# Logits of a mixture-of-experts gate from eight extra columns of the output projection, in a decoder block on one Trainium2 core

## The reference

```python
y = _layer_norm(x + _mha(x, Wqkv, bqkv, Wo, bo), g1, be1)
z = _layer_norm(y + _moe(y, Wg, W1, b1, W2, b2), g2, be2)
...
logits = xf @ Wg.T              # xf: the rows of y
idx = jnp.argmax(logits, axis=-1)
for e in range(E):
    m = (idx == e)[:, None].astype(xf.dtype)
    h = jax.nn.relu(xf @ W1[e] + b1[e])
    out = out + m * (h @ W2[e] + b2[e])
```

## Time and profile before

| | us |
|---|---|
| median of 3 runs | 1223.05 (1222.92 to 1227.51) |
| the profiled execution, its time | 1222.52 |
| the profiled execution, its span from the first to the last instruction | 1220.8 |
| TensorE busy in the span | 1124.4 (92%) |
| VectorE / ScalarE / GpSimd busy | 727.6 / 483.6 / 500.4 |
| mean granted TensorE clock | 0.983 of full speed |

### The profile page before, as it was taken

How to read it: one execution, slowest core, us unless ns; L and a number is a source line. 1 busy time by engine, 2 the same in 40 slices (tenths; PEclk the granted TensorE clock), 3 DMA queues, 4 the chain that set the end, 5 groups by cost and what they waited for, 6 DMA issues and landing times. The chain is left out here.

```text
span 1220.8 us, 29847 instructions
## 1 busy us (share of the span) xinstructions
PE 1124.4 (92%) x10228; PEld 768.5 (63%) x10237; DVE 727.6 (60%) x2056; ACT 483.6 (40%) x863; POOL 500.4 (41%) x721
## 2 busy tenths in 40 slices
PE   8999999999999999999898889888889999999995
PEld 3545455464554644645554455666657999999994
DVE  4555666757766677565725556554565655656553
ACT  5444454445454545445352233322213333333330
POOL 3334425244252443442432222343243566556664
PEclk9999999999999999999999999998979999999998
DMA  7266654644637345364372132348013111111110
GB/s 222 71 186 160 173 155 115 184 111 121 188 105 210 88 143 163 89 192 136 80 203 74 53 105 88 114 136 290 20 41 103 48 46 52 49 53 52 52 44 7
DMA packets 142614, 137.97 MB, mean 113 GB/s; under 512 B 29512, under 2 KB 135886, under 8 KB 142416
## 3 DMA queue, kind: packets, MB, share of 16 engines
q1 hardware_dynamic: 136944, 124.20, 35.4%
q0 software_dynamic: 5280, 12.66, 3.1%
q10 hardware_dynamic: 320, 0.16, 0.1%
HBM read 49.37 MB, written 50.83 MB: 82 GB/s over the span
## 5 line engine op out<-in xcount | busy, mean ns | idle before, releaser
L970 ACT ACTIVATE probs<-ps_ab 128x512 f32<-128x512 f32 (+2 forms) x352 | 174.5, 537 | 92.4 <-PE ps_ab L1292 36.5
L591 POOL TENSOR_SCALAR_AFFINE_SELECT probs<-probs 128x512 f32<-128x512 f32 x128 | 81.9, 640 | 267.0 <-ACT probs L970 263.0
L2810 PE MATMUL ps_ab<-e_yT,e_w_now 128*128 128x128 f32 x1248 | 145.8, 275 | 0.0
L2810 PEld LDWEIGHTS ps_ab<-e_yT,e_w_now 128*128 128x128 f32 x1248 | 142.5, 192 | 0.1
L2821 PE MATMUL ps_c<-keep_w,e_hT 128*128 x624 | 141.0, 379 | 0.0
L2821 PEld LDWEIGHTS ps_c<-keep_w,e_hT 128*128 128x128 f32 x624 | 115.7, 190 | 14.1
L712 DVE CUSTOM_DVE_ANT_0 ps_ab<-ps_ab,mask_qk 128x256 f32<-128x256 f32 x224 | 88.9, 450 | 18.9 <-PE ps_ab L1261 18.8
L706 DVE TENSOR_REDUCE top<-ps_ab 128x2 f32<-128x512 f32 (+1 forms) x112 | 74.1, 683 | 28.4 <-PE ps_ab L1261 27.5
L2745 DVE TENSOR_SCALAR e_hT<-ps_ab,keep_b 128x128 f32<-128x128 f32 x312 | 84.4, 343 | 7.5 <-PE ps_ab L2810 4.6
L1261 PE MATMUL ps_ab<-k_rows,q_rows 96*128 96x256 bf16 (+1 forms) x512 | 84.5, 260 | 4.6 <-DVE top L712 2.7
L1820 ACT ACTIVATE e_w_now<-keep_w 128x1024 f32 x78 | 78.1, 1049 | 22.2 <-issue 12.3
(11 more groups left out here) (236 smaller groups left out, 2120.8 us busy)
## 6 DMA issues: line engine op xcount, KB each, us to landing
sorted_rows<-filler SPq DMA_DIRECT2D x8, 4290.0 KB, 16.9
q_rows<-parts SPq DMA_DIRECT2D x96, 128.0 KB, 2.4
k_rows<-parts SPq DMA_DIRECT2D x96, 128.0 KB, 2.4
q_rows<-q_parts SPq DMA_DIRECT2D x96, 128.0 KB, 2.4
keep_w<-in_e_w SPq DMA_DIRECT2D x16, 512.0 KB
keep_w<-in_e_w SPq DMA_DIRECT2D x8, 1024.0 KB
e_row<-sorted_rows SPq DMA_DIRECT2D x39, 130.0 KB, 2.1
x_in<-in_x SPq DMA_DIRECT2D x8, 512.0 KB, 3.9
```

The costliest lines, as they stand in the source:

```text
L591: nc.gpsimd.affine_select(own, own, [[0, TILES], [1, P]], ALU.is_ge, keep_zero, base=0, channel_multiplier=-1).then_inc(probs_cut.sem, 1)
L970: nc.scalar.activation(probs[:, user % 2, lo:lo + width], ps_exp[:, f % 2, 0:width], ACT.Exp).then_inc(exp_done.sem, 1)
L2810: mm = nc.tensor.matmul(ps_h[s][:, f // 4, (f % 4) * P:(f % 4 + 1) * P], w1_now[:, s, k, f * P:(f + 1) * P], yT[:, s, k * P:(k + 1) * P], ...
```

## The change

The mixed rows are not transposed for the gate any more, and there is no product with m_w_g per group. Instead the matrices of the value projection and of the output projection get eight columns more (`GATED = 264`): `g1*Wg` beside the values' weights, and `Wo` times `g1*Wg` beside the output's. The projection of values thus gives `x @ (g1*Wg)` of the group as well, which `keep_gate` keeps beside x plus bias, and the output projection adds its own part. GpSimd's new `logits` makes the logits of them with mean and rstd. The extra columns are made at the start of mixing: `make_gates` on VectorE, `gate_weights` on TensorE, `take_gates` on ScalarE.

With 264 columns a bank holds one tile, so values and output each have four fills (v0 to v3, out0 to out3) instead of two, and four copies or adds. ScalarE's loop is now written out instead of run by a hardware loop, and the values have a buffer of their own.

The order moves too: TensorE does scores(n+1) right behind the values and ahead of ranks(n); VectorE does the slots of the group before, and the four adds, within the softmax, and the statistics of the group after next behind those of the post-norm; GpSimd makes the bias first and the other group's m_rstd last, and its row sends no longer wait for m_yT.

```diff
-ROUTE_FILLS = ["out0", "out1", "yT0", "yT1", "logits", "ranks"]
-HALVES_FILLS = ["out0", "out1", "yT0", "logits0", "yT1", "ranks0", "logits1", "ranks1"]
-PROJECT_FILLS = ["xT0", "xT1", "q0", "q1", "k0", "k1", "v0", "v1"]
-MIX_FILLS = ["xT0", "xT1", "out0", "out1", "q0", "q1", "k0", "k1", "yT0", "yT1", "v0", "logits", "v1", "ranks"]
+ROUTE_FILLS = ["out0", "out1", "out2", "out3", "ranks"]
+HALVES_FILLS = ["out0", "out1", "out2", "out3", "ranks0", "ranks1"]
+GATED = D + E
+PROJECT_FILLS = ["xT0", "xT1", "q0", "q1", "k0", "k1", "v0", "v1", "v2", "v3"]
+MIX_FILLS = ["xT0", "xT1", "out0", "out1", "out2", "out3", "q0", "q1", "k0", "k1", "v0", "v1", "v2", "v3", "ranks"]
...
+                "xT": (xT_ready, KD + k + 1), "q": (q_ready, KD + k + 1), "k": (k_ready, KD + k + 1),
+                "v": (v_ready, TILES + k + 1), "out": (mixed_ready, k + 1), "ranks": (next_row_ready, k + 1),
...
+                def logits(n, k, own):
+
+                    wide = [P, own.stop - own.start, E]
+                    pool.wait_ge(mixed_ready.sem, mixed_ready.count(n, own.stop))
+                    nc.gpsimd.tensor_tensor(logit[:, 0, own, :], moments1[:, own, 0:1].broadcast_to(wide),
+                                            gate_sums[:, 0:1, :].broadcast_to(wide), ALU.mult).then_inc(logit_steps.sem, 1)
+                    pool.wait_ge(logit_steps.sem, logit_steps.count(n, 4 * k + 1))
+                    nc.gpsimd.tensor_tensor(logit[:, 1, own, :], mixed[:, own, D:GATED], logit[:, 0, own, :],
+                                            ALU.subtract).then_inc(logit_steps.sem, 1)
+                    pool.wait_ge(logit_steps.sem, logit_steps.count(n, 4 * k + 2))
+                    pool.wait_ge(ln1_rstd.sem, ln1_rstd.count(n, k + 1))
+                    nc.gpsimd.tensor_tensor(logit[:, 2, own, :], logit[:, 1, own, :], rstd1[:, own].unsqueeze(2).broadcast_to(wide),
+                                            ALU.mult).then_inc(logit_steps.sem, 1)
+                    pool.wait_ge(logit_steps.sem, logit_steps.count(n, 4 * k + 3))
+                    nc.gpsimd.tensor_tensor(logit[:, 3, own, :], logit[:, 2, own, :], gate_sums[:, 1:2, :].broadcast_to(wide),
+                                            ALU.add).then_inc(logit_steps.sem, 1)
...
                     if ahead:
                         for h in range(2):
                             if n > 0:
-                                pool.wait_ge(mixed_ready.sem, mixed_ready.count(n, h + 1))
+                                pool.wait_ge(mixed_ready.sem, mixed_ready.count(n, 2 * h + 2))
                             bias(n + 1, h)
-                    if n == 0:
-                        return
-                    for k, own in enumerate(post_norm_parts(n)):
-                        post_norm_rstd(n, k, own)
-                    number_rows(n)
+                    if n > 0:
+                        for k, own in enumerate(post_norm_parts(n)):
+                            post_norm_rstd(n, k, own)
+                            logits(n, k, own)
+                    if more:
+                        ln_first(n + 2)
+                    if n > 0:
+                        number_rows(n)
...
                 for n in range(2, NGROUPS):
                     iteration(n, ahead=n < NGROUPS - 1, more=n < NGROUPS - 2)
-                    if n < NGROUPS - 1:
...
+                    if i == 0:
+                        dve.wait_ge(gate_kept.sem, gate_kept.count(n, 0))
                     ps = work_take(dve, n, f"out{i}")
-                    nc.vector.tensor_tensor(mixed[:, 2 * i:2 * i + 2, :], ps.rearrange("p (c d) -> p c d", c=2),
-                                            xnb[:, (n - 1) % 2, 2 * i:2 * i + 2, :], ALU.add).then_inc(mixed_ready.sem, 1)
+                    nc.vector.tensor_tensor(mixed[:, i, :], ps[:, 0:GATED], xnb[:, (n - 1) % 2, i, :], ALU.add
+                                            ).then_inc(mixed_ready.sem, 1)
+
+                def make_gates():
+
+                    for k in range(KD):
+                        scaled_by_norm = w_qkv[:, k, 3 * D:3 * D + E]
+                        nc.vector.tensor_scalar(scaled_by_norm, w_g[:, k, :], g1_column[:, k:k + 1], None, ALU.mult).then_inc(gates_made.sem, 1)
+                        nc.vector.tensor_scalar(gates[:, k, 0, :], w_g[:, k, :], g1_column[:, k:k + 1], None, ALU.mult).then_inc(gates_made.sem, 1)
+                        nc.vector.tensor_scalar(gates[:, k, 1, :], w_g[:, k, :], be1_column[:, k:k + 1], None, ALU.mult).then_inc(gates_made.sem, 1)
+                        nc.vector.tensor_scalar(gates[:, k, 2, :], w_g[:, k, :], g1_column[:, k:k + 1], b_o_column[:, k:k + 1],
+                                                ALU.mult, ALU.mult).then_inc(gates_made.sem, 1)
+
+                def keep_gate(n):
+
+                    dve.wait_ge(v_ready.sem, v_ready.count(n, TILES))
+                    if n == 0:
+                        dve.wait_ge(gates_ready.sem, 3)
+                    nc.vector.tensor_tensor(xnb[:, n % 2, :, D:GATED], v[:, :, D:GATED],
+                                            gate_sums[:, 2:3, :].broadcast_to([P, TILES, E]), ALU.add).then_inc(gate_kept.sem, 1)
...
                 def iteration(n, more=True):
                     route = n > 0
                     shift_scores(n)
+                    if n > 1:
+                        slots(n - 1, whole, 0, "ranks")
+                    if route:
+                        mix(n, 0)
+                    sum_up(n)
+                    if route:
+                        mix(n, 1)
+                        mix(n, 2)
+                    normalise(n)
+                    if route:
+                        mix(n, 3)
+                    turn(n)
+                    keep_gate(n)
+                    if route:
+                        post_norm_statistics(n, whole)
                     if more:
                         ln_statistics(n + 2)
-                    normalise(n)
-                    turn(n)
                     if route:
-                        mix(n, 0)
-                        mix(n, 1)
-                        post_norm_statistics(n, whole)
                         post_norm_scale(n, whole)
                         post_norm_apply(n, 0, whole)
+                        choose(n, whole, 0)
                     if more:
                         ln_apply(n + 2)
-                    if route:
-                        choose(n, whole, 0, "logits")
-                        slots(n, whole, 0, "ranks")
...
+                def values(n):
+                    if n >= 0:
+                        act.wait_ge(gate_kept.sem, gate_kept.count(n, 1))
+                    for c in range(TILES):
+                        ps = work_take(act, n, f"v{c}")
+                        nc.scalar.activation(v[:, c, :], ps[:, 0:GATED], ACT.Copy).then_inc(v_ready.sem, 1)
+
+                def take_gates():
+
+                    act.wait_ge(gates_summed.sem, 1)
+                    nc.scalar.activation(w_o_back[:, :, :], ps_heads[:, 0, :].rearrange("p (j n) -> p j n", j=KD),
+                                         ACT.Copy).then_inc(gates_ready.sem, 1)
+                    act.wait_ge(gates_summed.sem, 2)
+                    nc.scalar.activation(w_o[:, :, D:GATED], ps_heads[:, 1, 0:KD * E].rearrange("p (k e) -> p k e", k=KD),
+                                         ACT.Copy).then_inc(gates_ready.sem, 1)
+                    nc.scalar.activation(gate_sums[:, :, :], ps_heads[:, 2, 0:3 * E].rearrange("p (i e) -> p i e", i=3),
+                                         ACT.Copy).then_inc(gates_ready.sem, 1)
...
+                def projected_values(n):
+                    for c in range(TILES):
+                        ps = work_claim(pe, n, f"v{c}")
-                    mm.then_inc(work_full.sem, 1)
+                            mm = nc.tensor.matmul(ps[:, 0:GATED], xT[:, k, c * P:(c + 1) * P], w_qkv[:, k, 2 * D:2 * D + GATED],
+                                                  start=(k == 0), stop=(k == KD - 1), skip_group_check=True)
+                        mm.then_inc(work_full.sem, 1)
+
+                def gate_weights():
+
+                    for j in range(KD):
+                        for k in range(KD):
+                            mm = nc.tensor.transpose(ps_heads[:, 0, (KD * j + k) * P:(KD * j + k + 1) * P],
+                                                     w_o[:, k, j * P:(j + 1) * P], identf[:, :])
+                    mm.then_inc(gates_summed.sem, 1)
+                    pe.wait_ge(gates_made.sem, 4 * KD + 1)
+                    for k in range(KD):
+                        nc.tensor.matmul(ps_heads[:, 2, 0:3 * E], ones, gates[:, k, :, :].rearrange("p i e -> p (i e)"),
+                                         start=(k == 0), stop=(k == KD - 1), skip_group_check=True)
+                    pe.wait_ge(gates_ready.sem, 1)
+                    for k in range(KD):
+                        for j in range(KD):
```

(26 more changed lines are left out.)

180 lines of the change are left out of this document (71 added, 109 removed).

## The result

The changed kernel takes 1216.45 us (median of 8 runs, 1213.11 to 1219.66), the kernel before 1223.67 us (8 runs). The ratio is 0.9944 with a 95% interval from 0.9929 to 0.996: 7 us gained, where 22 were forecast (1201.5 us), and outside the range of 1191 to 1213. The profiled execution has a span of 1211.3 us and a time of 1213.34 us, 9.5 us of span less than the one before.

The account below looks back on a forecast made before the run. TensorE's queue was taken to set the mixing stage's pace. Loop 18.5 + after q/k(6) 7.6 - start 4.3 - tail 0.3 = 21.5 us gained: 1201.0 us for the profiled execution, median 1201.5, range 1191 to 1213.

Parts of the forecast that it names:

- the period: Mixing loop, one q/k projection to the next: 25.30 us falls to 21.2, taken as 21.3 for holes in the scores.
- m_next_row's 0.96: Loop, second transpose group: a new TensorE wait of 0.96 us until VectorE's m_next_row frees the bank of ranks.
- The 3.6 us left in for the burst of expert weights: Loop: one period disturbed during the expert weight loads was 3.6 us longer before; that cost was kept in.
- Rival 4: Loop: no change, as a hole each period brings the 1.2 GHz clock and loses 20 to 25 us; 1223 us, chance 0.05.
- The six loads: Attention part: six more small loads, column forms of three vectors, issued with the other constants, costed at nothing.
- The start: Start of mixing to the end of q/k(1): 1.3 us of lateness plus 3.0 of slow clock, 4.3 us lost.
- The wait for the copy: Start of mixing: TensorE idles 5.9 us before the gate products, whose ScalarE copy stands behind m_mask_pos.
- q/k(6) to the last scores: After the loop: heads 1.55, values 3.96, scores 2.7 make 8.2 us instead of 11.5, gain 3.3.
- from there to the output projection: Last scores to the last group's output projection: VectorE sets 13.2 us instead of 17.5, gain 4.3.
- waits for m_mixed: Loop, ahead of q/k: TensorE's wait of 1.37 us for m_mixed goes, by two moves in VectorE's order.
- inside their cover: Loop: GpSimd's four logit operations, 0.25 us each plus gaps, 1.25 in all, with 7.5 us of cover.
- tail and experts: After the last output projection: GpSimd's row sends delay m_rstd and the logits, so nothing is gained, -0.3 us.

Follow-up runs that it names:

- the dose: Eighteen small column loads, read by nothing, added at the end of the constants in the kernel before: 1233.47 us, ratio 1.0077.
- One moved line: Changed kernel with ScalarE's copies of the gate sums moved ahead of its wait for the position mask: 1208.14 us, ratio 0.9879.
- the sends first: Changed kernel with GpSimd's row sends at the head of the next iteration, not at its tail: 1200.83 us, ratio 0.9823.
- the one with six loads: Kernel before with six small column loads, read by nothing, added at the end of the constants: 1221.5 us, ratio 1.002.
- all three edits: Changed kernel with row sends at the iteration's head, six column loads issued later, gate copies ahead of the mask wait: 1188.69 us, ratio 0.9752.
- the plain sends: Changed kernel with each indirect send replaced by a plain transfer to a fixed place, without sorting by expert: 1196.85 us, ratio 0.981.
- slots first: Kernel with row sends, column loads and gate copies moved, plus VectorE's slots ahead of shifting the scores: 1187.89 us, ratio 0.9738.
- the later plain sends: Changed kernel with plain sends to fixed places and six additions ahead of them, so they fall beside the scores: 1196.38 us, ratio 0.9776.

## Why the prediction was wrong

**The failed step** is the period: "I take 21.3, since some periods hold a hole of about 1 us within the scores that nothing releases". I had read those holes as a given of the scores and costed them at a flat 0.1 us a period. In the changed kernel they belong to GpSimd's indirect sends, and the change moved the sends. In the text on GpSimd I wrote that the sends "no longer wait for m_yT but stand behind them" and counted only GpSimd's own time, 12 of 21 us. The trace of before had a hint: the four runs of the scores that overlap a send have holes, the four without are whole. Comparing the two kinds would have raised the question. Without the holes the period is 19.9, below the forecast 21.3; with them and the slow clock behind them 23.3 on average (one period of 19.6 ahead of the first sends, four of 23.8 to 24.8). The period's own sum (less by waits and transposes, more by m_next_row's 0.96) was right, but its base was not: the 25.30 us held 1.3 us of holes and their after-effects, and from the 24.0 without them the same sum gives 19.9. The wait for m_next_row came at 0.42 to 1.11 us.

The 3.6 us left in for the burst of expert weights did not come: the changed kernel has no hole of 2 us in its loop. So the loop's 116.6 us, forecast 110.1, are 10 us more than five periods of 21.3, and luck took 3.6 off the miss.

**Rival 4**, the one through the clock, named the right mechanism with the wrong trigger. It asked for one hole of 2.08 us and set "the largest hole left in a period is 0.96" against it. Here several holes of 0.4 to 1.2 us in a row came ahead of the slow stretches; in the first such period none was over 0.59 us. It got 0.05.

**The six loads** "I cost them at nothing": 3.1 us by the dose. I looked at who uses the data, not at what stands behind the issues on their queue. I had said that a wait would be for six issues there, and gave it no price.

**The start** was forecast as -4.3 and came at -1.9 in the profiles, by parts that were off both ways: q/k(-1) came 15.4 us after the stage's first instruction and not 12.9, and the rest ran faster than my chain of durations. The wait for the copy was foreseen (5.9 us, measured 5.45), but I priced its lateness at 1.3 us and the rest as clock. One moved line gains 8.3 us by the medians and 6.1 in the profiles, with keep_warm as slow as before, so it was the wait that cost.

**Right as worked out:** q/k(6) to the last scores (8.4 us, forecast 8.2), from there to the output projection (13.0, forecast 13.2) with its wait for m_chosen:

```profile
885.30 0.18 PE L2564 MATMUL ps_d<-m_chosen,m_before 128*128 128x32 bf16 x1 [5.01 <-DVE m_chosen L2268]
```

TensorE waits for m_mixed ahead of q/k no more, and GpSimd's m_logit operations take 0.23 to 0.51 us, inside their cover: no group in the loop waits for m_chosen. By the rule of the Trainium skill (SBUF — State Buffer, two separate sides) each could have waited out a VectorE operation of 0.42 us; of the 28 in this trace four are more than 0.05 us over the shortest of their kind, by at most 0.26 us, and it cost nothing. In the tail m_rstd does stand behind six sends and VectorE waits 2.07 us for it; tail and experts lost 2.4 us instead of 0.3, and what the other 2.1 are is not traced:

```profile
891.76 0.96 POOL L2116 DMA_INDIRECT sorted_rows<-m_rows,m_slot  x1 [0.31 <-issue]
892.75 0.21 POOL L2081 TENSOR_TENSOR m_veps<-m_moments,m_eps 128x2 f32<-128x2 f32 x1
893.03 0.73 POOL L2083 TENSOR_TENSOR m_rstd<-m_veps,m_half 128x2 f32<-128x2 f32 x1
```

## What to carry to other kernels

When a change moves an engine's DMA issues, look at what TensorE does at their old and new place, not only at whether the issuing engine has time. Holes "that nothing releases" should be lined up against the other engines' rows before they are taken as noise: compare the repeats that have them with those that don't, and look for the same alignment in every other profile before calling it the cause. Price a new load by what stands behind it on its queue; and after a change of this kind try the order of its small parts, for three moved pieces were worth three times the change itself.

## What the hardware did that was not expected

Indirect sends by GpSimd beside a run of small TensorE matmuls (64x32) went with holes in it: 0.2 to 1.2 us each, three or four beside the two to three sends that overlap a run in the changed kernel, and one or two beside the one send of the kernel before. Neither additions by GpSimd nor its plain sends of the same rows brought them, and beside matmuls of 264 and 512 columns four indirect sends left none (818.79 to 823.70 us with the sends first). In one of the three profiles of the kernel before with a send beside the scores, the one with six loads, there was none either.

Holes of 2.1 and 2.3 us in all were followed by some 7 us at 1.2 GHz, holes of 1.8 and 2.1 by a shorter stretch (0.76 on average over 7 us), and holes of 1.2 by none. The disturbed periods took 3.9 to 4.9 us more than 19.9.

A lone hole of 0.4 to 1.2 us stands at a fixed place of TensorE's program: in the seventh run of the scores it lies behind 75 of the 128 matmuls in all six forms of the changed kernel without indirect sends beside the scores (it ends between 823 and 839 us). Where the third run has one it lies behind 101 (with all three edits, and with the plain sends), and in the fifth behind 88 (slots first, and the later plain sends): 13 matmuls earlier every two runs. A hole that stays at one instruction while its time and the load around it change, and that moves on by a fixed count from run to run, points to the program's text and not to another engine; no run tested it.
